# A graph layer on one core: message-passing batches of 42-node ranges, in pairs that share a PSUM bank, with the one-hots made three batches ahead

## What is computed

```python
# 3 edge types t, 3 steps i each; src, dst: 50000 edges, sorted by dst
m   = h @ W[i]
msg = m[src] * emask[:, None]            # emask: the edge is of type t
agg = segment_sum(msg, dst, num_segments=N)
gi, gh = agg @ wih.T + bih, h @ whh.T + bhh
r = sigmoid(i_r + h_r); z = sigmoid(i_z + h_z); n = tanh(i_n + r * h_n)
h = (1 - z) * n + z * h
```

## Time and profile before

| | us |
|---|---|
| median of 3 runs | 2778.94 |
| lowest, highest | 2778.64, 2779.45 |
| span of the profiled execution | 3036.4 |
| its own time | not shown apart from the span |
| busy in the span: PE, DVE, POOL, ACT | 2646.3, 1592.0, 1358.7, 642.5 |
| graph convolution in the span | about 600 to 2485 |

### The profile page before, as it was taken

One profiled execution on the slowest core, in us unless ns is written; L12 is line 12 of the kernel. 1 busy time (PEld: TensorE's weight loads), 2 busy tenths in 40 slices (PEclk: granted clock), 3 DMA queues, 4 the chain that ended last, 5 costly groups with the idle time before them and its releaser, 6 DMA issues. The chain is left out here.

```text
span 3036.4 us, 39301 instructions
## 1 busy us (share of the span) xinstructions
PE 2646.3 (87%) x13041; PEld 1701.2 (56%) x13041; DVE 1592.0 (52%) x3119; ACT 642.5 (21%) x1180; POOL 1358.7 (45%) x1375
## 2 busy tenths in 40 slices
PE   5898899779988898798899996898888966999997
PEld 3434455465555556554455554654545556788886
DVE  6798777445555554355555552466766784011110
ACT  3211000111111114111111123122212221332232
POOL 0000500066666661666666634666666600333333
PEclk7899999889999999899999998899999985999998
DMA  4300766334444443444444434343444423133223
GB/s 129 132 1 1 286 240 218 117 104 129 144 144 137 138 135 104 126 125 145 128 129 145 145 97 157 118 121 112 123 129 124 122 58 100 35 90 92 65 64 72
DMA packets 201473, 362.85 MB, mean 120 GB/s; under 512 B 27937, under 2 KB 156109, under 8 KB 201104
## 3 DMA queue, kind: packets, MB, share of 16 engines
q0 software_dynamic: 67776, 169.95, 20.2%
q1 hardware_dynamic: 129564, 186.48, 18.4%
q10 hardware_dynamic: 3956, 4.19, 0.5%
HBM read 293.37 MB, written 70.34 MB: 120 GB/s over the span
## 5 line engine op out<-in xcount | busy, mean ns | idle before, releaser
L1453 POOL DMA_INDIRECT xnT<-h_rows,idx x780 | 775.2, 994 | 378.0 <-issue 206.6
L1124 PEld LDWEIGHTS g_pagg<-g_onehot,xnT 128*128 128x128 f16 x4680 | 337.1, 99 | 408.3 <-issue 396.3
L1124 PE MATMUL g_pagg<-g_onehot,xnT 128*128 128x144 f16 x4680 | 416.0, 230 | 154.8 <-issue 152.8
L1295 DVE TENSOR_TENSOR g_agg<-g_agg,g_pagg 128x288 f32 x585 | 265.1, 453 | 370.6 <-remote 159.6
L1453 POOL DMA_INDIRECT xnT<-xn_rows,idx x366 | 360.6, 985 | 198.8 <-issue 95.0
L1298 DVE SCALAR_TENSOR_TENSOR g_onehot<-iota_keys,shift,keys 128x288 f16<-128x288 f16 x585 | 299.1, 513 | 0.6 <-DVE g_pre_at L1287 0.3
L1201 PE MATMUL g_pr<-g_agg,g_wc 128*128 128x448 f32 (+1 forms) x576 | 231.1, 520 | 18.1 <-DVE g_agg L1295 9.1
L1387 DVE SCALAR_TENSOR_TENSOR g_t<-g_ph,g_bh,g_rT 128x448 f32<-128x448 f32 (+1 forms) x144 | 89.8, 624 | 282.3 <-remote 199.1
L1201 PE MATMUL g_pz<-g_hT,g_wh 128*128 128x448 f32 (+1 forms) x576 | 224.4, 509 | 9.9 <-issue 5.9
L1201 PE MATMUL g_pz<-g_agg,g_wc 128*128 128x448 f32 (+1 forms) x576 | 228.8, 520 | 1.1 <-issue 0.9
L1201 PE MATMUL g_pr<-g_hT,g_wh 128*128 128x448 f32 (+1 forms) x576 | 224.8, 512 | 3.7 <-issue 3.5
(11 more groups left out here) (356 smaller groups left out, 3371.7 us busy)
## 6 DMA issues: line engine op xcount, KB each, us to landing
ma_R<-q_cols SPq DMA_DIRECT2D x27, 896.0 KB, 12.0
f_w<-in_L_ffn_W SPq DMA_DIRECT2D x16, 1024.0 KB, 7.7
h_cols<-g_hn SPq DMA_DIRECT2D x36, 448.0 KB
h_rows<-g_rows SPq DMA_DIRECT2D x36, 448.0 KB
g_hT<-h_cols SPq DMA_DIRECT2D x36, 448.0 KB
mix_R<-q_cols SPq DMA_DIRECT2D x15, 896.0 KB, 9.6
xnT<-h_rows,idx POOLq DMA_INDIRECT x780
ma_R<-q_cols SPq DMA_DIRECT2D x9, 1120.0 KB, 5.9
```

The costliest lines, as they stand in the source:

```text
L1124: mm = e.matmul(pg[:, k * TYPES:(k + 1) * TYPES, :].rearrange("p t d -> p (t d)"), rows[:, c, o:o + P], hot[:, c, :], start=(c == 0 and pa ...
L1295: e.tensor_tensor(agg[:, :, bass.ds(o, DT)], agg[:, :, bass.ds(o, DT)], pagg[b % BANKS][:, :, :], ALU.add).then_inc(S["added"], 1)
L1453: e.indirect_dma_start(ring[:, b % SLABS, c, :], None, tables[s], bass.IndirectOffsetOnAxis(ap=idx[:, o:o + 1], axis=0)).then_inc(landed[b ...
```

## The change

DT becomes 42, so NKEY 126: a count matmul streams 126 columns, a one-hot has 252 elements and an add 252. The division by DT at L297 to L299 is done with other constants. The result of a batch then takes 1008 of a bank's 2048 bytes, and two batches share each of the three banks (HALVES = 2, SUMS = 6). A bank is handed over as a whole: before an even batch b PE waits for the adds of b - 6 and b - 5, before an odd one for no add. DVE adds in pairs: in the place of an even batch b it adds b - 4 and b - 3, when both are counted; in that of an odd batch none. DVE makes one-hots three batches ahead (AHEAD = 3), in seven buffers in place of four. KEPT is 4: by the planner groups 2 to 7 begin with one batch more done (28, 52, 80, 109, 138, 167 in place of 27, 51, 79, 108, 137, 166), and what a group waits for is what the pairs have added by then: 8, 24, 48, 76, 106, 134, 164, 195 batches, before 9, 24, 48, 76, 105, 134, 163, 195. The widest batch, 33 nodes, still fits.

```diff
-DT = 48
+DT = 42
-BANKS, KEPT, SURE = 3, 3, 1
+BANKS, HALVES, KEPT, SURE = 3, 2, 4, 1
+SUMS = BANKS * HALVES
+AHEAD, HOTS = 3, 7
...
+def added_by(b):
+
+    if b == MB - 1:
+        return MB
+    whole = PLAN[0] // HALVES * HALVES if b >= PLAN[0] - 1 else 0
+    return max(0, b // HALVES * HALVES - HALVES, whole)
 def batches_needed(g):
-    return MB if g == NG - 1 else PLAN[GPU * NU * g] - (KEPT if g else 0)
+    return MB if g == NG - 1 else added_by(PLAN[GPU * NU * g] - 1)
...
-        onehot = sb("onehot", [P, 4, BATCH, NKEY], F16)
+        onehot = sb("onehot", [P, HOTS, BATCH, NKEY], F16)
-        pagg = [ps(f"pagg{i}", [P, KC * TYPES, DT]) for i in range(BANKS)]
+        pbank = [ps(f"pagg{i}", [P, HALVES, KC * TYPES, DT]) for i in range(BANKS)]
+        pagg = [pbank[i // HALVES][:, i % HALVES, :, :] for i in range(SUMS)]
...
         def pe_range(e, s, first, end):
             for b in range(first, end):
                 e.wait_ge(S["onehot"], s * MB + b + 1)
-                if b >= BANKS:
-                    e.wait_ge(S["added"], s * MB + b - BANKS + 1)
+                if b >= SUMS and b % HALVES == 0:
+                    e.wait_ge(S["added"], s * MB + b - SUMS + HALVES)
                 e.wait_ge(landed[b % SLABS], landings(s, b))
-                count_batch(e, pagg[b % BANKS], ring[:, b % SLABS, :, :], onehot[:, b % 4, :, :], S["batch"])
+                count_batch(e, pagg[b % SUMS], ring[:, b % SLABS, :, :], onehot[:, b % HOTS, :, :], S["batch"])
...
         def dve_add(e, s, b):
             o = e.value_load(main_at[0:1, b + 1:b + 2], min_val=0, max_val=NP)
-            e.wait_ge(S["batch"], s * MB + b + 1)
+            e.wait_ge(S["batch"], s * MB + min(MB, b // HALVES * HALVES + HALVES))
...
         def dve_batches(e, s, p):
             for b in range(batches_before(p - 1), batches_before(p)):
-                if b >= BANKS and not PLAN[0] <= b < PLAN[0] + BANKS:
-                    dve_add(e, s, b - BANKS)
+                for i in range(added_by(b - 1), added_by(b)):
+                    dve_add(e, s, i)
                 if b == 0:
-                    dve_onehot(e, s, 0)
-                if b + 1 < MB:
-                    dve_onehot(e, s, b + 1)
-                if b in (PLAN[0] - 1, MB - 1):
-                    for i in range(BANKS):
-                        dve_add(e, s, b - BANKS + 1 + i)
+                    for i in range(AHEAD):
+                        dve_onehot(e, s, i)
+                if b + AHEAD < MB:
+                    dve_onehot(e, s, b + AHEAD)
```

More of the change, by code:

```diff
@@ L296, in dve_edges @@
             step(e.tensor_copy(most_i[:, :], most[:, 0:1]))
-            step(e.tensor_scalar(most_i[:, :], most_i[:, :], 4, None, ALU.logical_shift_right))
-            step(e.tensor_scalar(most_i[:, :], most_i[:, :], 171, None, ALU.mult))
-            step(e.tensor_scalar(most_i[:, :], most_i[:, :], 9, None, ALU.logical_shift_right))
+            step(e.tensor_scalar(most_i[:, :], most_i[:, :], 1, None, ALU.logical_shift_right))
+            step(e.tensor_scalar(most_i[:, :], most_i[:, :], 3121, None, ALU.mult))
+            step(e.tensor_scalar(most_i[:, :], most_i[:, :], 16, None, ALU.logical_shift_right))
             step(e.tensor_copy(most[:, 1:2], most_i[:, :]))
@@ L1282, in dve_pre @@
                     e.wait_ge(V[s]["batch"], r * NB + b + 1)
-                    e.tensor_tensor(agg[:, :, bass.ds(o, DT)], agg[:, :, bass.ds(o, DT)], pagg[0][:, :, :], ALU.add).then_inc(V[s]["added"], 1)
+                    e.tensor_tensor(agg[:, :, bass.ds(o, DT)], agg[:, :, bass.ds(o, DT)], pagg[0], ALU.add).then_inc(V[s]["added"], 1)
                     e.wait_ge(V[s]["added"], r * NB + b + 1)
@@ L1291, in dve_add @@
             o = e.value_load(main_at[0:1, b + 1:b + 2], min_val=0, max_val=NP)
-            e.wait_ge(S["batch"], s * MB + b + 1)
+            e.wait_ge(S["batch"], s * MB + min(MB, b // HALVES * HALVES + HALVES))
             if b:
                 e.wait_ge(S["added"], s * MB + b)
-            e.tensor_tensor(agg[:, :, bass.ds(o, DT)], agg[:, :, bass.ds(o, DT)], pagg[b % BANKS][:, :, :], ALU.add).then_inc(S["added"], 1)
+            e.tensor_tensor(agg[:, :, bass.ds(o, DT)], agg[:, :, bass.ds(o, DT)], pagg[b % SUMS], ALU.add).then_inc(S["added"], 1)
         def dve_onehot(e, s, b):
-            e.scalar_tensor_tensor(out=onehot[:, b % 4, :, :], in0=iota_keys[:, :].unsqueeze(1).to_broadcast([P, BATCH, NKEY]), scalar=shift[:, 0:1],
+            e.scalar_tensor_tensor(out=onehot[:, b % HOTS, :, :], in0=iota_keys[:, :].unsqueeze(1).to_broadcast([P, BATCH, NKEY]), scalar=shift[:, 0:1],
                                    in1=keys[:, BATCH * (b + 1):BATCH * (b + 2)].unsqueeze(2).to_broadcast([P, BATCH, NKEY]), op0=ALU.add, op1=ALU.is_equal).then_inc(S["onehot"], 1)
```

## The result

The changed kernel takes 2804.44 us (median of 4 runs, 2801.07 to 2806.05) against 2779.19 in the same session: ratio 1.0089, 95% interval 1.0077 to 1.0102. It is 0.9% slower, and 92 us above the forecast of 2712.

The account below looks back on a forecast made before the run. The prediction took PE's stream to bound the kernel. Gains of 30 (columns), 38 (more sums) and 3 (group 1), less 2 of costs, made 69; less 2 lost on the way, 2778.9 - 67 = 2712 us, range 2675 to 2750.

Parts of the forecast that it names:

- The bound: Graph convolution steps: PE's stream sets the pace, with PE busy 2646.3 of 3036.4 us in the profile.
- B: PE's waits for adds at batch starts: six sums give two batches more slack, gaining 38 us, ends 5 and 90.
- A, columns: PE's count matmuls: 126 columns instead of 144 start every 56 ns instead of 62, gaining 30 us.
- rival 3: PE's count matmuls: weight loads bound them, so fewer columns gain 0 and more sums still help; 2745 us, chance 0.05.
- Pairs: DVE's order: two adds at even places, none at odd, mostly covered by idle time; cost 1 us, ends 0 and 20.
- Group starts: Starts of planned groups: group 1 gains 3 us by needing 8 adds, not 9; group 2's extra batch costs 1.
- DVE's work: DVE's adds and one-hots: 38 ns shorter each, 44 us less work beside PE's, worth 0 on the path.
- Rival 2: POOL's gathers take over as the bound, with a floor of 534 us a step; 2740 us, chance 0.14.
- Rival 5: DVE's order: the pair's second add delays unit work, reaching ACT and PE; slower, 2801 us, chance 0.05.

Follow-up runs that it names:

- e1: The kernel before the change, unchanged and profiled a second time: 2781.1 us, ratio 1.0002.
- e2: The kernel before the change with DT 42 alone (126 columns): 2777.6 us, ratio 0.9990.
- e5: The changed kernel with KEPT 3 and one add in each batch's place instead of pairs: 2777.6 us, ratio 0.9994.
- e3: The changed kernel with KEPT 3, so the old plan of group starts: 2799.5 us, ratio 1.0068.
- e13: The changed kernel with one-hots left out from the eighth batch of the first step on (sums wrong): 2770.8 us, ratio 0.9962.
- e9: The kernel before the change with KEPT 4 alone: 2786.3 us, ratio 1.0022.

## Why the prediction was wrong

**The bound (failed step).** "So the graph convolution goes at PE's pace" was read from one disturbed execution. The runs show POOL's gathers in its place. In e1 POOL goes through each step's gathers without a pause (503.4 us of the 549.9 of step 2), and PE waits for landings; 33 us less work on PE gave 2.6 (e2), and after is slower by what its gathers and its tail grew. The late batch starts with an add 0.1 us before them, on which B rests, are not there: all waits ahead of count matmuls come to 35.4 us, 33.9 of them for landings, and of 19 over 0.45 us none has an add ending within 0.15 us before it. The sign that something was off was at hand, the span 9.3% over the median. The prediction halved B for it, but kept the bound that the same rows suggested.

**A, columns.** The size was right, or a little small: 8 matmuls in 0.61 us with a last one of 0.22 are (0.61 - 0.22) / 7 = 56 ns apart, as forecast. The gain of 30 us was hidden (e2: 2.6). The spacing fell from 62 ns, so loads did not pace it there, and rival 3 falls for its reason. (Its own sum gives 2743, not 2745.) Whether loads or columns pace it at 56 isn't shown.

**B, more sums.** 38 us forecast, nothing found: e5, with six sums, takes the time of e2, with three, since there is nothing left to cover. Its count was off as well. In the trace of before 49 batches, not 57, start over 0.45 us late, 83.3 us together, and another 64 such stops lie inside batches, where nothing is waited for. They are of the kind that the prediction saw in the earlier trace rows and took for a sign of the profile alone.

**Pairs.** Cost 1 with ends 0 and 20; measured 22 (e3 against e5). The step looked at who waits for DVE, and e13 shows no cost of that kind. It did not ask what stands next to what, and so put the effect on the gathers at nothing. It also had the second add of a pair at 0.45 us. It starts 0.82 us behind the first, as DVE's timeline and its waits after show; that its wait for the first add and the read of its base are no longer hidden is my explanation for it. (The rows are from the adds in front of the first unit; over all 300 neighbouring adds the median is 0.83.)

```profile
1157.08 0.42 DVE L1306 TENSOR_TENSOR g_agg<-g_agg,g_pagg 128x252 f32 x1 [0.20 <-DVE g_agg L1306]
1157.90 0.42 DVE L1306 TENSOR_TENSOR g_agg<-g_agg,g_pagg 128x252 f32 x1 [0.40 <-DVE g_agg L1306]
```

```profile
DVE g_agg L1306 <- DVE g_agg L1306: 97.8, 265, 0.9
```

**Group starts.** Forecast a gain of 2; measured a cost of 5 to 8 (e3, e9, the line above). "Moves 0.5 us of counting earlier, not more work" holds for PE's work. But the last batch moves earlier as well, and what is behind it grows by 3.1 us a step, while POOL's last gather sets when that batch can start.

**DVE's work.** Adds 37 ns shorter, one-hots 39, against 38 each: right, and worth nothing, as said.

**The rivals.** Rival 2 named the true bound, and the reading given for it came out: no wait for slabs beyond the usual gap within a step's gathers, PE idle at fresh landings. Its floor of 534 us a step stands against 549.9 in e1, so 16 us were to spare, not 106, and 13 of those are long gathers (503.4 against 390 x 1.26 = 491). Its 2740 was no better than the forecast, since it still took the slack from the disturbed profile. Rival 5 had the sign and nearly the time (2801), by luck: its mechanism, the second add reaching ACT and PE, is the one that e13 speaks against.

## What to carry to other kernels

Where the profiled execution's span is far from the median, profile the same kernel again before reading any wait from it; here a second profile would have moved the bound from PE to POOL. Where GpSimd issues back-to-back gathers and paces the kernel, judge every edit of VectorE's order by what VectorE does when a gather starts, and above all by runs of instructions with two SBUF operands. Here an operand given as a scalar of each partition, a short instruction between, or the order of two neighbours was worth more than VectorE's own time. A plan that finishes the shared resource's work earlier in another engine's order lengthens the tail behind it.

## What was not expected of the hardware

A gather of 128 rows that takes 0.95 us alone took up to 2.32 us (after, at 756.74) beside DVE's instructions. Of 12144 gathers that started while DVE was idle or in an add, reset product or candidate's input, one lasted over 1.15 us; of 2601 that started in a difference, weighing or new state, 1099 were. One-hots that cost DVE 30 to 48 us more made kernels 9 to 26 us faster. Two adds of 0.42 us right behind each other on DVE start 0.82 us apart. And the first profiled execution of the kernel before, on one core, was 265 us (9.6%) longer than the second.
